# Expert blocks of 256 and 128 rows, and a one-hot with the tile index innermost

## What is computed

```
layer 0:  8 experts, k = 2, hidden 512,  gelu
layer 2:  8 experts, k = 2, hidden 256,  gelu
layer 3:  8 experts, k = 1, hidden 1024, relu, at most ceil(1.25 * 6250 / 8) rows an expert

y = act(x @ w1[e] + b1[e]) @ w2[e] + b2[e]
out += weight[node, e] * y
```

```
z = h @ W_func.T
e = leaky_relu(concat(z[src], z[dst], edge_attr) @ W_att.T)
m = segment_max(e, dst);  e_exp = exp(e - m[dst])
agg = segment_sum(e_exp / segment_sum(e_exp, dst)[dst] * z[src], dst)
```

## Time and profile before

| | |
|---|---|
| median of 3 runs | 8493.2 us (8480.46 to 8498.29) |
| the profiled execution | 8498.12 us, its span 8496.4 us |
| busy share of the span: TensorE, VectorE, ScalarE, GpSimd | 71%, 62%, 37%, 61% |
| mean granted TensorE clock, share of full | 0.837 |
| sparse experts of layer 0, about | 2266 to 2760 us of the span |
| attention loop of the third layer | 5897 to 7047 us |
| sparse experts of layer 2, about | 7297 to 7561 us |
| sparse experts of layer 3, about | 7997 to 8490 us |

### The profile page before, as it was taken

One profiled execution on the slowest core, in us unless ns is written; L12 is line 12 of the kernel. 1 busy time (PEld: TensorE's weight loads), 2 busy tenths in 40 slices (PEclk: granted clock), 3 DMA queues, 4 the chain that ended last, 5 costly groups with the idle time before them and its releaser, 6 DMA issues. The chain is left out here.

```text
span 8496.4 us, 115689 instructions
## 1 busy us (share of the span) xinstructions
PE 6033.3 (71%) x29315; PEld 4567.5 (54%) x29315; DVE 5274.7 (62%) x14255; ACT 3110.5 (37%) x9132; POOL 5222.3 (61%) x5183
## 2 busy tenths in 40 slices
PE   6586777774499555556798888955677774673599
PEld 5234555553387233433677777744455553552487
DVE  9867888887664676665544444446677767345544
ACT  1245888887322200000433333312444444222322
POOL 0475666665577677777777777746777762424322
PEclk9798999996699777777699998867888885786699
DMA  5475666653365333333111111116333343663364
GB/s 145 153 249 157 172 175 172 171 169 108 116 206 177 119 101 102 101 100 95 23 27 32 31 27 31 26 38 189 104 103 104 104 87 124 189 199 81 124 199 163
DMA packets 636527, 1018.18 MB, mean 120 GB/s; under 512 B 137746, under 2 KB 439330, under 8 KB 634540
## 3 DMA queue, kind: packets, MB, share of 16 engines
q0 software_dynamic: 243360, 540.20, 24.0%
q1 hardware_dynamic: 392588, 471.25, 17.6%
HBM read 793.10 MB, written 225.75 MB: 120 GB/s over the span
## 5 line engine op out<-in xcount | busy, mean ns | idle before, releaser
L4281 POOL DMA_INDIRECT gat_edges_rows<-gat_table,gat_room x1080 | 1120.8, 1038 | 355.8 <-issue 316.9
L2825 POOL DMA_INDIRECT l_edges_ring<-pairs,first_room x832 | 842.6, 1013 | 473.9 <-issue 244.1
L2387 POOL DMA_INDIRECT l_sum_rows<-l_feats,back_room x832 | 828.2, 995 | 266.1 <-issue 242.8
L2407 PE MATMUL l_sum_o<-l_sum_rows,l_sum_s 128*128 128x256 f32 x1664 | 606.9, 525 | 467.4 <-DVE l_sum_s L2418 204.6
L2876 ACT ACTIVATE l_edges_ring<-l_edges_ring,l_edges_weight 128x64 f32<-128x64 f32 x3328 | 816.6, 336 | 0.0
L2407 PEld LDWEIGHTS l_sum_o<-l_sum_rows,l_sum_s 128*128 128x128 f32 x1664 | 408.8, 260 | 658.8 <-DVE l_sum_s L2418 295.9
L2948 PE MATMUL l_edges_o<-l_edges_ring,l_edges_sf 128*128 128x260 f32 x1664 | 536.4, 428 | 149.6 <-DVE l_acc L3081 142.4
L3890 ACT ACTIVATE m_ffn_ht<-m_ffn_hp,m_ffn_b1t 128x256 f32<-128x256 f32 x592 | 280.0, 473 | 873.5 <-PE m_ffn_hp L3858 872.2
L2429 DVE TENSOR_TENSOR l_acc<-l_acc,l_sum_o 128x256 f32 x832 | 349.9, 420 | 352.6 <-PE l_sum_o L2407 264.4
L3868 PE MATMUL m_ffn_yp<-m_ffn_w2b,m_ffn_ht 128*128 128x256 f32 x2368 | 546.7, 384 | 28.4 <-ACT m_ffn_ht L3890 27.5
L3858 PE MATMUL m_ffn_hp<-m_ffn_xt,m_ffn_w1b 128*128 128x256 f32 x2368 | 548.2, 385 | 8.5 <-DVE m_ffn_xt L3905 5.1
(11 more groups left out here) (869 smaller groups left out, 14685.1 us busy)
## 6 DMA issues: line engine op xcount, KB each, us to landing
sorted_rows<-l_proj_zero SPq DMA_DIRECT2D x44, 1032.0 KB
m_ffn_xs<-sorted_rows SPq DMA_DIRECT2D x144, 258.0 KB, 3.6
m_ffn_w1b<-in_L_ffn_w SPq DMA_DIRECT2D x32, 1024.0 KB, 5.9
m_ffn_w2b<-in_L_ffn_w SPq DMA_DIRECT2D x32, 1024.0 KB, 5.4
m_ffn_w1b<-in_L_ffn_W SPq DMA_DIRECT2D x56, 512.0 KB, 4.8
m_ffn_w2b<-in_L_ffn_W SPq DMA_DIRECT2D x56, 512.0 KB
m_by_node<-gat_edges_ys SPq DMA_DIRECT2D x96, 256.0 KB
l_proj_taken<-m_by_node SPq DMA_DIRECT2D x28, 768.0 KB, 7.0
```

Of the source, the lines that this page charges most:

```text
L2387: pool.indirect_dma_start(rows[:, slot, j, :], None, table, bass.IndirectOffsetOnAxis(ap=L.src[:, t:t + 1], axis=0)).then_inc(got[slot], 16)
L2407: pe.matmul(o[:, j, 0:D], s4[:, q % S4, j, :], rows[:, slot, j, :], start=True, stop=True).then_inc(out_done, 1)
L2825: pool.indirect_dma_start(rows(q, 0, 2 * D)[:, j, :], None, table, bass.IndirectOffsetOnAxis(ap=L.src[:, t:t + 1], axis=0)).then_inc(got[q ...
L4281: pool.indirect_dma_start(rows[:, slot, j, :], None, table, bass.IndirectOffsetOnAxis(ap=L.src[:, q * B + j:q * B + j + 1], axis=0)).then_ ...
```

## The change

Experts in blocks of two sizes. For k = 2 there are 48 blocks of 256 rows and then 9 of 128 rows (57 blocks, 13440 rows; before 56 blocks, 14336 rows). For k = 1 there are 24 and then 8 (32 blocks, 7168 rows; before 32 blocks, 8192 rows). `table` rounds each expert's rows up to 128, gives the pairs of tiles to the full blocks in the order of the experts, and what is left to the half blocks; it issues 36 small instructions on one partition, before 17. In a half block each engine does the work of 128 rows; the weights are loaded whole. The attention loop's one-hot gets bfloat16 operands and the tile index innermost, its readers therefore read with a step of 8 elements, and the ring loses one place. Code that nothing called is removed (`route`, `dispatch`, `mixture`).

```diff
@@ edge_softmax
-    RO = 5
+    RO = 4
...
-        s8 = ph.sb("s8", [P, U, B, P], BF16)
+        s8 = ph.sb("s8", [P, U, P, B], BF16)
+        names = ph.sb("names", [P, P, B], BF16)
+        dst_b = ph.sb("dst_b", [P, L.tiles], BF16)
...
-                    act.activation(far[:, q % 2], s8[:, slot], ACT.Identity, bias=minus_far[:],
+                    act.activation(far[:, q % 2], s8[:, slot].rearrange("p k q -> p q k"), ACT.Identity, bias=minus_far[:],
...
-                        act.activation(ws[:, q % 2, j, :], s8[:, slot, j, :], ACT.Identity,
+                        act.activation(ws[:, q % 2, j, :], s8[:, slot, :, j], ACT.Identity,
...
-                        ins = pe.transpose(stp[:, j, :], s8[:, slot, j, :], core.ident_b[:])
+                        ins = pe.transpose(stp[:, j, :], s8[:, slot, :, j], core.ident_b[:])
...
-                dve.wait_ge(begun, 5)
+                dve.tensor_copy(names[:], bc(core.row[:], 2, [P, P, B])).then_inc(begun, 1)
+                dve.tensor_copy(dst_b[:], L.dst).then_inc(begun, 1)
+                dve.wait_ge(begun, 7)
...
-                    dve.tensor_tensor(s8[:, slot], bc(core.row[:], 1, [P, B, P]),
-                                      bc(L.dst[:, q * B:(q + 1) * B], 2, [P, B, P]), ALU.is_equal).then_inc(s_ready, 1)
+                    dve.tensor_tensor(s8[:, slot], names[:], bc(dst_b[:, q * B:(q + 1) * B], 1, [P, P, B]),
+                                      ALU.is_equal).then_inc(s_ready, 1)
@@ runs_of
-    runs = (k * N + experts * (S2 - 1)) // S2
-    return runs + runs % 2
+    full = k * N // S2 // 4 * 4
+    half = max(experts, (k * N + experts * (P - 1)) // P - 2 * full)
+    return full, half
...
@@ experts
+    blocks = lambda q: 2 if not fixed(q) or q < full else 1
...
-                    sp.dma_start(xs[:, par], sorted_rows[ds(row, S2), :].rearrange("(h p) d -> p h d", p=P)
+                    sp.dma_start(xs[:, par, 0:n], sorted_rows[ds(row, n * P), :].rearrange("(h p) d -> p h d", p=P)
...
-                steps(sp, runs, [(0, load)])
+                steps(sp, runs, [(0, load)], tail=half)
...
-                    for h in range(2):
+                    for h in range(blocks(q)):
                         pool.indirect_dma_start(by_node, bass.IndirectOffsetOnAxis(ap=home[:, slot, h:h + 1], axis=0),
...
-                            ins = pe.matmul(hp[:, k % HB, 0:S2], w1b[:, par, c, k * P:(k + 1) * P], xt[:, par, c, :],
+                            ins = pe.matmul(hp[:, k % HB, 0:n], w1b[:, par, c, k * P:(k + 1) * P], xt[:, par, c, 0:n],
...
-                    for h in range(2):
+                    for h in range(blocks(q)):
                         for k in range(HC):
                             ins = pe.matmul(yp[:, par, h, :], ht[:, par, k, h * P:(h + 1) * P], w2b[:, par, k, :],
```

More of the change, by code:

```diff
@@ L3217, in __init__ @@
         self.E, self.K, self.name = experts, k, name
-        self.runs = runs_of(experts, k)
+        self.full, self.half = runs_of(experts, k)
+        self.runs = self.full + self.half
         self.weight = weight
@@ L3273, in open @@
         self.cmp = sb("cmp", [1, R.runs, E])
-        self.nt, self.ends, self.ones_e = [sb(n, [1, E]) for n in ("nt", "ends", "ones")]
+        self.nt, self.ends, self.ones_e, self.whole, self.half_ends, self.step, self.begun = [
+            sb(n, [1, E]) for n in ("nt", "ends", "ones", "whole", "half_ends", "step", "begun")]
         self.nti = ph.sb("route_nti", [1, E], I32)
@@ L3514, in table @@
-        o.then(dve.tensor_copy(self.run_f, self.run_i[:]))
[L3515 to L3520, removed]
+        A, B = R.full, R.half
@@ new lines, in table @@
+        wide = lambda ap, n: bc(ap, 2, [1, n, E])
+        each = lambda ap, n: bc(ap, 1, [1, n, E])
+        nt, ends, whole, half_ends, step, begun = self.nt, self.ends, self.whole, self.half_ends, self.step, self.begun
+        o = Own(dve, self.own_t, 48).at(0)
+        dve.wait_ge(self.put_ready, T // CH)
+        o.then(dve.tensor_scalar(nt, self.sofar[0:1, :], P - 1.0, None, ALU.add))
+        o.then(dve.tensor_copy(self.nti[:], nt))
+        o.then(dve.tensor_scalar(self.nti[:], self.nti[:], 7, None, ALU.logical_shift_right))
@@ new lines, in table @@
+        o.mark(dve.tensor_scalar(begun, whole, float(S2), None, ALU.mult))
+        o.then(dve.tensor_copy(self.run_f, self.run_i[:]))
+        o.then(dve.tensor_scalar(self.run_f[:, A:], self.run_f[:, A:], -float(A), None, ALU.add))
+        for lo, n, end, size in ((0, A, ends, whole), (A, B, half_ends, step)):
+            at = slice(lo, lo + n)
+            o.then(dve.tensor_tensor(self.cmp[:, at], wide(self.run_f[:, at], n), each(end, n), ALU.is_ge))
+            o.then(dve.tensor_reduce(self.where[:, at], self.cmp[:, at], AX.X, ALU.add))
+            o.then(dve.tensor_tensor(self.cmp[:, at], self.cmp[:, at], each(size, n), ALU.mult))
+            o.then(dve.tensor_reduce(self.begin[:, at], self.cmp[:, at], AX.X, ALU.add))
@@ L3735, in experts @@
     HC = HID // P
-    runs = R.runs
+    runs, full, half = R.runs, R.full, R.half
+    assert full % G4 == 0
+    blocks = lambda q: 2 if not fixed(q) or q < full else 1
+    sent = lambda q, par: full * 16 + (q - par - full) * 8 if fixed(q) and q > full else (q - par) * 16
+    brought = lambda q, slot: full * 8 + (q - slot - full) * 4 + 16 if blocks(q) == 1 else (q - slot) * 8 + 32
     with Phase(nc, f"{R.name}_ffn") as ph:
@@ L3829, in _ @@
                 else:
-                    steps(pool, runs, [(0, store)] if onto is None else [(0, gather), (2, store)], unroll=G4)
-                pool.wait_ge(y_out[0], 16 * runs)
-                pool.wait_ge(y_out[1], 16 * runs)
+                    steps(pool, runs, [(0, store)] if onto is None else [(0, gather), (2, store)], unroll=G4,
+                          tail=half)
+                for par in range(2):
+                    pool.wait_ge(y_out[par], 16 * full + 16 * len(range(full + par, runs, 2)))
             @block.tensor
@@ L3849, in up @@
                 def up(q, par):
+                    n = blocks(q) * P
                     pe.wait_ge(xt_ready, q + 1)
@@ L3875, in _ @@
                 else:
-                    steps(pe, runs, [(0, turn), (1, up), (2, down)])
+                    steps(pe, runs, [(0, turn), (1, up), (2, down)], tail=half)
             @block.scalar
@@ L3896, in _ @@
                 else:
-                    steps(act, runs, [(1, activate)])
+                    steps(act, runs, [(1, activate)], tail=half)
             @block.vector
@@ L3953, in _ @@
                     return
[L3954 to L3966 removed]
+                steps(dve, runs, [(0, copy_x), (0, find_home), (2, finish)], unroll=G4, lead=4 if onto is None else runs + 2,
+                      tail=half)
 def first_routing(core, experts):
[L3971 removed]
+    runs = sum(runs_of(experts, 2))
     later = core.weight[1][0:1].rearrange("o t k -> o (t k)").bitcast(I32)
```

269 lines of the change are left out of this document (46 added, 223 removed).

## The result

The changed kernel takes 8415.7 us (median of 4 runs, 8405.6 to 8422.9) beside 8495.8 us for the kernel before (4 runs, 8480.5 to 8505.2): a ratio of 0.9908, 95% interval 0.9895 to 0.992, or 68 to 89 us less. The forecast of 8410 us and its range of 8390 to 8445 us hold. The parts of the sum hold less well, and that is the subject of what follows.

What follows compares the result with a forecast made beforehand. GpSimd's gather issue was taken to set the attention loop, and TensorE, DMA or GpSimd the expert stages. Terms -24 - 48 - 5 - 6 = -83 gave 8415 us for the profiled execution, 8410 for the median; range 8390 to 8445.

Steps and rivals of the forecast that it cites:

- The one-hot: Attention loop: 104 VectorE instructions go from 1.22 to 0.68 us and disturb gathers less; -24 us, bounds 0 and -30.
- Two copies at the head: Head of the attention loop: copies of names and destinations run beside gathers four blocks ahead; 0, or +2 if GpSimd is held.
- Ring of 10: Attention loop: a gather waits for the collect of block q - 10, with time to spare; 0, bound +3 us.
- Readers with a step: Attention loop: TensorE pays 0.4 us a step, ScalarE nothing to +1.1, both staying below the gathers; 0.
- rival C: Attention loop: stepped reads make ScalarE the bound from 3.5 times per element; at four times 8528 us; chance 0.05.
- Layer 3: Layer 3's experts: half blocks take 9.2 instead of 14.74 us, -44, and a shorter end, -3.5; together -48 us.
- The tail of -3.5: End of layer 3's experts: VectorE's finish has half the elements and one store of 1.3 us goes; -3.5 us.
- Rival B: All three expert stages: weight transfers bind half blocks, 11 us each in layer 3, nothing gained elsewhere; 8436 us, chance 0.18.
- Layer 2: Layer 2's experts: 8 blocks fewer at 4.5 us, 9 half blocks at 3.5; -5 us, bounds +2 and -14.
- Layer 0: Layer 0's experts: GpSimd has 353 instead of 360 DMAs, half blocks need 7.0 us; -6 us, bounds 0 and -12.
- Tables: Routing tables on VectorE: 19 more instructions, +3.8 us three times, stay covered in layer 3; otherwise +4 each.
- Rival A: Attention loop: the gathers aren't relieved, so the loop gives 0; 8434 us, chance 0.15.

## Why the prediction came out right

**The one-hot (-24): right.** The time of 0.68 us, the relief of 26 us and the mechanism (a long gather is one that finds the one-hot running) all hold; gathers over 1.0 us fell from 97 to 22. With the waits mended, the loop is those 26 us shorter.

**Two copies at the head (0, at most +2): wrong, +13.4.** The step that failed is "beside gathers that run four blocks ahead". I had priced the copies by their own length and looked at what they overlap, but not at what stands ahead of them on VectorE: with nothing between memset and copy, the hold on GpSimd reached back over the memset.

**Ring of 10 (0, at most +3): wrong.** Alone it costs 13 us of waits, in the changed kernel 11 to 19. The failed step is the spare of "0.6 us at the least and 1.9 in the middle", set against a need of nothing. The spare itself was too large: it was read off the adds, and taking the usual 0.96 us between a collect and its add off each gives 0.54 and 1.9. But where TensorE is late the add follows the collect by 0.15 us only. Read from the collects, the least spare of those 92 pairs is -0.19 us, and 11 of them have 0.27 us or less. And the need is not nothing: a gather that waits starts 0.78 us behind its collect. With half a block's grace every gather but the last block's has 3.3 us or more behind the collect that it then needs, and no wait is left. I set the last two pairs aside as slow landing, though the last alone costs 3 us.

**Readers with a step (0): the cost right, its size low.** TensorE's load came to 151 ns where 148 was forecast. ScalarE's bound of half as much again was too low: +1.0 us a step for `far` and 8 x 0.12 for the tiles, 2.0 us in all where +1.1 was the bound. It stays hidden, as making `far` straight again showed; rival C's 3.5 times is far off.

**Layer 3 (-48): -59, and +6.5 at the end.** The mis-sized term is the up product's: 4.5 us for 32, taken from 8 in 1.13 us. In a run of 32 they take 3.57 (8353.53 to 8357.10), half of the full ones; a group of 8 taken by its own 1.13 us overstates it. The 9.2 us was also a compromise with transfers that don't bind: 7.85 us is TensorE's sum, 3.57 + 3.56 + 0.72. The tail of -3.5 is right (4.7 us from the last finish to the store, 8.2 before to the second store). The +6.5 was foreseen by no term. Rival B is out: half the weights changed nothing here.

**Layer 2 (-5): right,** -5.5 in the mean of nine executions against four, at 3.6 to 4.0 us a half block where I had put 3.5. **Layer 0 (-6): -9,** within its bounds. From 2300 to 2500 us TensorE is busy for 191.8 of 200 us and GpSimd's 149 instructions at a pitch of 1.30 us come to 194, so both are full as I had read; the 7 DMAs fewer (9.1 us) give the measured 9.4, and my discount to 6 was one too many. **Tables (0): right,** 231.3 and 231.0 us, 256.9 and 256.0 us from the routing's start to its last put.

The sum was -83; the measured parts are 0 - 52 - 5.5 - 9 = -67. Of the 24 us that the loop kept back, 8 were made up by experts that gave more, and some 13 by the gap between these parts and the measured -80, whose interval begins at -68; the profiled execution had 11 us of it in layer 1's gathers. By the measured parts alone the changed kernel would take 8426 to 8429 us (67 less than 8493.2 or 8495.8), within the stated range and above the forecast. Rival A had the loop at 0, as it came out, though not for A's reasons: the gathers were relieved. So the range rests on sound parts, but that the forecast is within 6 us is luck. The time was right; the loop's share in it was not.

## What to carry to other kernels

When instructions are added at the head of a stage, look at what they are queued behind, not only at what they run beside: a copy with no wait ahead of it can take GpSimd's gathers away for as long as its predecessor runs, and one wait, or another order, gives them back. A place taken off a ring has to be priced from the work that frees it, with the distance at which the next user can follow (0.78 us here), and for the last blocks too; waiting for half a block can cost nothing and be worth more than the place. And when a change has several parts in stages with barriers between them, judge it by the stage lengths, since a total can come out right for reasons that cancel.

## What the runs showed of the hardware

- A gather was held 14.37 us by a memset of 10.55 us followed directly by two copies, 0.98 us with a semaphore wait between them, 1.29 us with the copies first.
- ScalarE reads bfloat16 with a step of 8 elements at 2129 ns for 1024 elements instead of 1145, and 512 instead of 388 ns for 128; TensorE's weight load takes 148 to 151 instead of 97 to 103 ns.
- A VectorE comparison of 1024 bfloat16 elements takes 685 ns with all operands stepping by one, 1218 ns with one operand standing still innermost, the same as float32.
- 16 float32 products (32 rows of the program) with 128 moving columns take 3.57 us, from the first's start to the next instruction's, and with 256 they take 6.9 (8451.09 to 8457.99): hardly any price for the short form in a long run.
- A gather that waits for a collect starts 0.78 us behind the end of its last product; in every twelfth block the second gather starts 3.59 us behind it or later (seven traces).
- One execution of the same code differs from the next by up to 23 us in layer 1's gathers, and by up to 19 us between them and the attention loop.
